# A graph kernel whose row and key comparisons read their ramp from PSUM instead of SBUF

## What is computed

```python
for l in range(3):
    X = einsum('ne,ref->rnf', out, weights[l])       # 9 products of all nodes
    msg = X[edge_type, src] + biases[l][edge_type]
    out = segment_sum(msg, dest)                     # relu after layers 0 and 1
x = layernorm(x + out)
alpha = cosine(x[row], x[col]) * beta                # softmax over the edges of a row
out = segment_sum(softmax(alpha) * x[col], row)
return layernorm(x + out)
```

## Time and profile before

| what | value |
|---|---|
| median of 3 runs | 5676.5 us (5673.23 to 5679.72) |
| the profiled execution, its time | 5667.57 us |
| its span | 5665.5 us, 68647 instructions |
| mean granted TensorE clock | 0.723 of full speed |
| TensorE matmul, busy | 3123.5 us (55%) |
| VectorE, busy | 2460.1 us (43%) |
| ScalarE, busy | 858.2 us (15%) |
| POOL, busy | 2704.9 us (48%) |

### The profile page before, as it was taken

How to read it: one execution, slowest core, us unless ns; L and a number is a source line. 1 busy time by engine, 2 the same in 40 slices (tenths; PEclk the granted TensorE clock), 3 DMA queues, 4 the chain that set the end, 5 groups by cost and what they waited for, 6 DMA issues and landing times.

```text
span 5665.5 us, 68647 instructions
## 1 busy us (share of the span) xinstructions
PE 3123.5 (55%) x13926; PEld 2003.1 (35%) x13927; DVE 2460.1 (43%) x9525; ACT 858.2 (15%) x1992; POOL 2704.9 (48%) x2839
## 2 busy tenths in 40 slices
PE   7112996555555555655555455556555533333698
PEld 4001553333333333333333333333333333322476
DVE  9101885333333333533333333334333322222699
ACT  2002991100010010000010001000001000000365
POOL 1774004555555555255555555552555566666100
PEclk9555997777777777877767777777777755555799
DMA  4000001222222222612212222216212121111454
GB/s 146 3 1 3 0 0 32 56 61 52 52 63 54 52 55 62 135 48 57 52 52 63 53 53 58 61 51 138 51 50 57 48 69 43 43 42 43 100 190 155
DMA packets 447303, 340.20 MB, mean 60 GB/s; under 512 B 263666, under 2 KB 404522, under 8 KB 447112
## 3 DMA queue, kind: packets, MB, share of 16 engines
q0 software_dynamic: 90368, 165.49, 12.5%
q1 hardware_dynamic: 153512, 113.25, 6.5%
q10 hardware_dynamic: 203360, 60.73, 4.4%
HBM read 232.12 MB, written 107.13 MB: 60 GB/s over the span
## 4 chain that ended last, share of the span: by engine, by line
another core or an unknown queue 41%; PE 18%; issue 16%; DVE 12%; DMA 5%; ACT 4%; DVEq 4%; ACTq 1%; POOL 0%; SPq 0%; POOLq 0%
PE ps L931 6%; PE ps L961 4%; PE ps L952 3%; DVE region L547 3%; DMA edge_absent<-region 2%; DVE oh L464 2%; DVEq L290 2%; DMA edge_counts<-region 2%; PE ps L1000 2%; PE ps L1028 2%; ACT ps L1077 1%; ACT region L1088 1%; DVE region L479 1%; DVE region L350 1%
## 5 line engine op out<-in xcount | busy, mean ns | idle before, releaser
L860 POOL DMA_INDIRECT region<-x_of_type,pair x2520 | 2399.8, 952 | 2365.9 <-PE ps L952 1035.6
L952 PE MATMUL ps<-oh,region 128*128 128x102 f32 x5040 | 1197.8, 342 | 1580.7 <-DVE region L547 1440.7
L961 PE MATMUL ps<-region 128*128 128x510 f16 x4200 | 1607.8, 461 | 536.2 <-issue 407.3
L952 PEld LDWEIGHTS ps<-oh,region 128*128 128x128 f32 x5040 | 1166.7, 256 | 2080.9 <-DVE region L547 1579.0
L464 DVE TENSOR_SCALAR oh<-iota_w,pair 128x102 f32<-128x102 f32 x2528 | 701.2, 278 | 2608.6 <-remote 1718.8
L961 PEld LDWEIGHTS ps<-region 128*128 128x128 f16 x4200 | 494.0, 124 | 779.7 <-issue 767.6
L547 DVE TENSOR_TENSOR region<-region,ps 128x102 f32 x2520 | 647.7, 257 | 13.5 <-issue 13.4
L1088 ACT COPY region<-ps 128x510 f32<-128x510 f32 x155 | 89.8, 580 | 3405.6 <-remote 1974.8
L931 PE MATMUL ps<-region 128*128 128x420 f16 x2016 | 392.4, 356 | 322.8 <-issue 259.4
L842 POOL DMA_INDIRECT scattered_edges<-region x304 | 300.6, 989 | 209.4 <-DVE ends L408 109.2
L931 PEld LDWEIGHTS ps<-region 128*128 128x128 f16 x2016 | 196.7, 99 | 519.0 <-issue 310.0
(11 more groups left out here) (179 smaller groups left out, 1546.2 us busy)
## 6 DMA issues: line engine op xcount, KB each, us to landing
region<-x_of_type,pair POOLq DMA_INDIRECT x2520
edge_counts<-region ACTq DMA_DIRECT2D x155, 255.0 KB
arrays<-edge_counts SPq DMA_DIRECT2D x40, 960.0 KB, 4.8
x_of_type<-region SPq DMA_DIRECT2D x50, 576.0 KB, 7.0
edge_absent<-region ACTq DMA_DIRECT2D x155, 127.5 KB
region<-edge_absent SPq DMA_DIRECT2D x40, 480.0 KB
x_of_type<-x0st SPq DMA_DIRECT2D x51, 192.0 KB
scattered_edges<-region POOLq DMA_INDIRECT x304
```

What stands on the lines that cost most here:

```text
L860: pool.indirect_dma_start(out=grow[:, u % GR, :], out_offset=None, in_=xt, in_offset=bass.IndirectOffsetOnAxis(ap=idx[:, u % GR:u % GR + 1 ...
L952: pe.matmul(ps[:, 6 + n % 2, t * RB:(t + 1) * RB], grow[:, u % GR, :], oh[:, u % U, 0:RB], start=True, stop=True).then_inc(s_used, 1)
L961: mm = pe.matmul(ps[:, c, 0:CW], cl[:, q % CR, c * P:(c + 1) * P], cr[:, q % CR, :], start=False, stop=False, skip_group_check=True)
```

## The change

The ramps that VectorE compares against move to bank 5 of PSUM, and so do some zeros. `one_hot` reads the f32 ramp there and `cell_hots` the fp16 one. The copies of indices and of keys, which had one input, become two-input operations (`bitwise_or` and `add`) whose second input is the zeros in PSUM, so that the result is the same. The sort's comparisons (L436, L437) keep their SBUF ramp.

Filling bank 5 is new work at the head of each layer. POOL makes a table `steps_down` at the start of the program, TensorE transposes five blocks of it into the bank (`turn_steps`), and VectorE then copies the f32 ramp and clears the zeros (`load_lanes`).

```diff
+        LANE_Z = RB + CG * P // 2
+        lane_r = ps[:, 5, 0:RB]
+        lane_h = ps[:, 5, RB:LANE_Z].bitcast(F16)
+        lane_zero = ps[:, 5, LANE_Z:LANE_Z + 2 * HALVES]
...
+            def load_lanes(l):
+                dve.wait_ge(s_ln, 1 + l)
+                nc_.tensor_copy(lane_r, iota_r)
+                step(nc_.memset(lane_zero, 0.0))
+
             def one_hot(u):
-                ins = nc_.tensor_scalar(oh[:, u % U, 0:RB], iota_r, rowb[:, u % GR:u % GR + 1], None, ALU.is_equal)
+                ins = nc_.tensor_scalar(oh[:, u % U, 0:RB], lane_r, rowb[:, u % GR:u % GR + 1], None, ALU.is_equal)
...
             def put_idx(t, h):
 
-                nc_.tensor_copy(pair[:, :, h * HALVES:(h + 1) * HALVES],
-                                arrays[:, 0:2, bass.ds(t, HALVES)].bitcast(I32)).then_inc(s_idx, 1)
+                nc_.tensor_tensor(pair[:, :, h * HALVES:(h + 1) * HALVES],
+                                  arrays[:, 0:2, bass.ds(t, HALVES)].bitcast(I32),
+                                  lane_zero.bitcast(I32).rearrange("p (n u) -> p n u", n=2),
+                                  ALU.bitwise_or).then_inc(s_idx, 1)
 
             def put_keys(k):
 
-                nc_.tensor_copy(keyc[:, :, :], arrays[:, 6:8, bass.ds(k, CB)]).then_inc(s_kc, 1)
+                nc_.tensor_tensor(keyc[:, :, :], arrays[:, 6:8, bass.ds(k, CB)],
+                                  lane_zero[:, 0:2 * CB].rearrange("p (n u) -> p n u", n=2), ALU.add).then_inc(s_kc, 1)
 
             def cell_hots(q, keys):
-                nc_.tensor_scalar(cl[:, q % CR, :], iota_h[:, :], keys[0], None, ALU.is_equal)
-                nc_.tensor_scalar(cr[:, q % CR, :], iota_h[:, 0:CW], keys[1], None, ALU.is_equal).then_inc(s_co, 1)
-
-
+                nc_.tensor_scalar(cl[:, q % CR, :], lane_h, keys[0], None, ALU.is_equal)
+                nc_.tensor_scalar(cr[:, q % CR, :], lane_h[:, 0:CW], keys[1], None, ALU.is_equal).then_inc(s_co, 1)
+
+
+            load_lanes(0)
             dve.wait_ge(s_srt, 16)
...
                     step(ins)
+                    load_lanes(l)
                 full = min(TURNS, CTURNS - TURNS * l)
...
-            nc_.iota(iota_h[:, :], pattern=[[1, CG * P]], base=0, channel_multiplier=0,
-                     allow_small_or_imprecise_dtypes=True).then_inc(s_pool, 1)
+            nc_.iota(steps_down[:, :].rearrange("p (b m) -> p b m", m=P), pattern=[[P, -(-NT // P)], [0, P]], base=0,
+                     channel_multiplier=1, allow_small_or_imprecise_dtypes=True).then_inc(s_pool, 1)
...
+            def turn_steps(bank, at, n):
+                for b in range(n):
+                    mm = pe.transpose(ps[:, bank, at + b * P // 2:at + (b + 1) * P // 2].bitcast(BF16),
+                                      steps_down[:, b * P:(b + 1) * P].bitcast(BF16), diag[:, P:2 * P])
+                mm.then_inc(s_ln, 1)
...
             pe.wait_ge(s_d, marks["digits"])
+            turn_steps(5, RB, CG)
...
                 if l:
                     pe.wait_ge(s_xe, XB + XQ * l)
+                    turn_steps(5, RB, CG)
```

More of the change, by code:

```diff
@@ L141, in gnn_program @@
         ones = sb("ones", [P, P])
-        iota_w = sb("iota_w", [P, CG * P])
-        iota_h = sb("iota_h", [P, CG * P], F16)
+        iota_w = sb("iota_w", [P, RB])
         x0st = sb("x0st", [P, X0 - 2, 3 * D])
@@ L148, in gnn_program @@
         blkt = arrays[:, 8, :].bitcast(I32)
+        steps_down = sb("steps_down", [P, -(-NT // P) * P], F16)
         endcol = sb("endcol", [P, 1])
@@ L219, in gnn_program @@
         ps = ctx.enter_context(nc.psum_tensor("ps", [P, 8, 512], F32))
+        LANE_Z = RB + CG * P // 2
+        lane_r = ps[:, 5, 0:RB]
+        lane_h = ps[:, 5, RB:LANE_Z].bitcast(F16)
+        lane_zero = ps[:, 5, LANE_Z:LANE_Z + 2 * HALVES]
+        assert LANE_Z + 2 * HALVES <= 512 and 2 * CB <= 2 * HALVES and CG * P <= NT
         s_edges = sem("s_edges")
@@ L268, in gnn_program @@
         s_sh = sem("s_sh")
+        s_ln = sem("s_ln")
         s_cl = [sem(f"s_cl{u}") for u in range(3)]
@@ L819, in _ @@
             nc_.memset(diag[:, :], 0.0).then_inc(s_pool, 1)
-            nc_.iota(iota_w[:, :], pattern=[[1, CG * P]], base=0, channel_multiplier=0,
+            nc_.iota(iota_w[:, :], pattern=[[1, RB]], base=0, channel_multiplier=0,
                      allow_small_or_imprecise_dtypes=True).then_inc(s_pool, 1)
```

## The result

The changed kernel takes 5839.7 us (median of 4, 5830.1 to 5846.3) against 5674.9 us (median of 4) for the one before: a ratio of 1.0288, 95% interval 1.0271 to 1.0306. The forecast was 5808 us, 2.3% slower; it came out 2.9% slower, inside the likeliest case's own range. Of all executions behind this document the ratios leave out one, which took 11825.8 us (the fourth of `early_psum`, twice the others). The span of the profiled execution grew from 5665.5 to 5838.2 us, 172.7 us.

The account below looks back on a forecast made before the run. VectorE's slot before the index copy, which POOL awaits because TensorE's signals are late, was taken as the bound. 141.5 + 4.5 - 13 + 2.3 = +135 us on 5667.6, about 5808 us expected; 8 in 10: 5685 to 6020 us.

Parts of the forecast that it names:

- the likeliest case: The forecast itself: longer slots make the whole kernel slower, about 5808 us, own range 5765 to 5855 us, chance 59%.
- the path: In the layers, one VectorE slot of each half turn, 2.72 us before the index copy, holds up POOL's next gather.
- the slot: VectorE's slot before the index copy: four one-hots and two pairs add 4 x 0.053 + 2 x 0.315 = 0.842 us.
- the rule that a longer stream moves all later starts by the whole difference: On VectorE, overlap between operations is a constant 0.09 us, so every added time counts in full for later starts.
- The choice between the bounds: Pairs' fp16 comparisons from PSUM: middle value 0.525 ns an element, between 0.251 and 1.047.
- Rival B: Pairs: fp16 from PSUM streams as from SBUF, only one-hots cost; +29 us, 5697 to 5706 us; 7%.
- rival C: Pairs: fp16 from PSUM streams as f32 does; +337 us, 6004 to 6013 us; 11%.
- 168 slots: Slots 1 and 4 of the 84 turns with cells, each 0.842 us longer: 141.5 us.
- Rival A: VectorE's comparisons make TensorE's signals late during POOL's gathers; the change ends POOL's waits, about 4621 us; 12%.
- The gathers: POOL's 2520 gathers lose 5 ns each if collisions with VectorE all vanish: 13 us come off.
- Rival D: Longer pauses drain more of TensorE's held signals, more groups find the copy earlier; +60 us, 5730 to 5740 us; 7%.
- The bank: Filling bank 5 behind the sort, transposes, copy and clearing: 2.3 us, once, fully on the path.

Follow-up runs that it names:

- early_psum: Changed kernel with the index copy moved to the start of the slot ahead; 5873.8 us, 1.0334 of the kernel before, without one execution.
- late_1_4: Kernel before, ramps in SBUF, plus four extra fp16 comparisons a turn in the slots before the index copies, late-signal chip; 5870.7 us, 1.0129.
- late_0_3: Kernel before, ramps in SBUF, plus four extra fp16 comparisons a turn in the slots behind the index copies, late-signal chip; 5805.0 us, 1.0014.
- after_again: Changed kernel unaltered, timed again beside the kernel before on another chip; 5843.3 us, 1.0278.
- repeat_1_4: Kernel before, ramps in SBUF, plus four extra fp16 comparisons a turn in the slots before the index copies, prompt-signal chip; 4280.8 us, 0.9988.
- moved_sbuf: Kernel before, ramps in SBUF, with the two pairs of slots 1 and 4 made in slots 2 and 5, behind the index copy; 5646.6 us, 0.9744.
- early_sbuf: Kernel before, ramps in SBUF, with the index copy moved to the start of the slot ahead; 5802.8 us, 1.0198 of the kernel before.
- only_pairs: Changed kernel with only the pairs' comparisons reading PSUM, one-hots and copies back on SBUF, prompt-signal chip; 4251.7 us, 0.9921 of the kernel before.

## Why the prediction was right, and where its sum was off

**Right: the path.** It named the slot ahead of the index copy as the only place of VectorE that counts. The profile after has the same pauses with a longer slot, and `late_1_4` against `late_0_3` shows it without PSUM. That holds for this order of work; with the copy moved ahead (`early_psum`) VectorE's comparisons cost time by another way.

**Mis-sized: the slot, 0.65 us and not 0.842.** The starts within the slots ahead of the copy (medians of 152 and 156 of them) tell which terms. A pair takes 0.288 us more to its successor's start, not 0.315: the fixed part is 207 ns for fp16 from PSUM and not the 224 that I kept, so L493 lasts 542 ns (560 forecast) and L494 474 (500). The four one-hots last 41 ns more each (319 ns, 331 forecast; fixed part 319 - 107 = 212), but put off what follows by 0.13 us together, not 0.21: the rule that a longer stream moves all later starts by the whole difference fails for two of them, whose additions start only 23 and 7 ns later. And what stands behind the four additions starts 0.06 us sooner, which the sum had at nothing. The choice between the bounds was right: I took 0.525 ns an element for fp16 from PSUM, and the two rows give 0.523. By the Trainium skill, "VectorE: DVE Perf Modes", section "Why PSUM operands drop a tier", this was the rate too; the trace now agrees. Rival B (0.251) and rival C (1.047) fall with it. VectorE's waking is 0.10 us later (2.44 against 2.34 us, medians), which I had not in the sum. The normal pause so grew by 0.71 us.

**Failed: "168 slots", each like the one of the earlier trace rows.** 40 of the 165 pauses with cells were short, 4.12 us on average, and I read only that there were 206 waits, not how long each was (1035.6 us over 206 is 5.0, well under 6.08, and could have told me). These places grew by 2.10 us each, 83.9 us, where 0.71 would be 28 us: some 55 us came from short pauses that turned normal. The smaller slot (some 30 us less than its term) took part of that back, so that the forecast is closer than its terms were; that much is luck. Why they turned is not settled. `after_again`, on another chip, has 5 short pauses as the first trace of the changed kernel has. It isn't PSUM as such: `late_0_3`, all in SBUF, has 7 short pauses on its chip. But that chip was slower for the kernel before as well (5799 us), and I have no trace of the unchanged kernel there. By the times its pauses sum to about 1238 us (an estimate: the 1244.1 us of `late_0_3` less the 6.2 us between the two), 124 us more than in the rows, so there most short pauses were probably gone without any change. Neither the length of the slot nor the chip is shown to be the cause.

**Rival A falls.** In the layers every comparison and copy of the change now has an operand in PSUM, and TensorE's signals stay as late: 1756.0 us of "remote" before one-hots, 10.08 us in the hand-over shown. And where signals are prompt, they are so beside comparisons that read SBUF in every group (`repeat_1_4`). So the source that VectorE reads does not make the signals late.

**The gathers: -20.7 us, not -13.** Not only the gathers held up above the median went (13 us); the median fell from 947 to 944 ns as well. Gathers over 970 ns were 237 and are now 5; the median need not be the change's, since `moved_sbuf` and `early_sbuf` have 944 ns with all ramps in SBUF. On the chips with prompt signals, where VectorE works during every gather, it was 28 to 32 us. The Trainium skill, "SBUF — State Buffer", section "Who interferes with whom", has VectorE's two-port operations and GpSimd block each other; the traces agree in kind and in both directions. One-hots from SBUF reach 496 ns in the kernel before and 518 in `only_pairs`, those from PSUM never more than 327; in size it is 1.3% of the gathers' time.

**Rival D** (longer pauses drain more, so that more groups find the copy early) is contradicted by waking 0.10 us later and by the short pauses, which became fewer (40 to 5). **The bank** took 1.1 us where I had 2.3. **The last addition:** 5803 and the 8.9 us between the runs and the profiled execution are 5812 us and not 5808; the slip changes nothing else.

## What to carry to other kernels

A slower operation costs where somebody waits for the slot it stands in, and here next to nothing elsewhere (6 us against 72, as long as the order of the work stays): find the hand-over, and move work behind it before making work cheaper. Here moving two pairs a slot gained 152 us on a chip with late signals. Putting the ramps in PSUM lost 165 us on another such chip; with prompt signals, the pairs alone gained 35 us, and all ramps, with the pairs moved, 28. Before pricing a pause by one example, take the distribution of all of them; and before moving a copy ahead, ask whether the engine it waits for is fed by the work that it overtakes.

## What the runs showed of the hardware that was not expected

One and the same kernel takes 4285 to 4286 us on two chips and 5675 to 5680 or 5799 us on others, while the gathers' 944 to 947 ns and POOL's 0.30 us between them are alike. The difference is in when other engines act on TensorE's work while POOL issues indirect DMAs: the first gather of the layers starts at 889 us on the one kind and at 555 in the kernels traced on the other, and pauses sum to over 1100 us in the kernel before against 63 (207 times 0.30). On the one kind 700 of the 10123 register and semaphore instructions of TensorE in the layers last over 0.3 us in the trace of the kernel before, 0.69 us on average, and 835 after; on the other none does in `only_pairs` and `repeat_1_4` (loads of a register from memory are left out of both counts). TensorE's granted clock goes with it and does not explain it: from 280 to 514 us it was 0.50 in the kernel before and 1.00 in `only_pairs`, but at the low one four matmuls of the sort take 1.58 us, while 11 us pass from one four to the next. What sets the kind of a chip no run here tells. The change is 2.8 to 2.9% slower on the first kind, while its larger part, the pairs, is 0.8% faster on the second, where the whole change was not run by itself; a verdict on such a kernel should say on which it was measured.
